# Reordering weight pieces, biases and operand copies around the middle of a two-layer fp32 kernel

## The chip, the cores and the metric

One core of a Trainium2 chip runs the whole program. The metric is the device time of one execution in microseconds (us), lower is better.

## The reference

```
x = x + ffn0(cond(x, c, W0c))      # cond: einsum('bct,bcd->bdt', x, W[c]), 64x64 matrices chosen by c
x = x + ffn1(cond(x, c, W1c))
ffn0(y) = y @ ternary(w) + b       # ternary(w) = where(|w| < 0.05, 0, sign(w)) * mean|w| of the column
ffn1(y) = y @ Wq.T + bias + 4 * (y @ A.T) @ B.T
Wq = NF4_LEVELS[q_weight] * q_scale          # one scale for 64 neighbours, 1024 x 1024
```

x is 32 x 64 x 1024 in fp32, `c` has 32 indices below 16, both weight matrices are 1024 x 1024, and A has 8 rows. Both layers run over the whole of x.

## The kernel before, in words

The 2048 rows of x are cut into NT = 16 tiles of 128 rows. Layer 0 handles tiles g = 0 to 15 and layer 1 handles the same tiles as g = 16 to 31. A tile passes through these steps:

- `mixed(g)`, 8 matmuls of 128 x 128 on TensorE that the trace shows as 16, multiplies the tile by its conditioning matrices and turns it, in two halves, into the PSUM tensor `xT`. There is one `xT` for almost all tiles, so `mixed(g+1)` waits until both halves of tile g have been read out of it.
- `high_x(g, h)` on ScalarE copies half h of it to SBUF in the reduced precision fp32r (`hh`), and `low_x(g, h)` on VectorE stores what that copy leaves over (`hl`, from PSUM minus `hh`). The two together are the left operand of the matmuls.
- `main(g, n)` on TensorE multiplies the operand by column half n of the weights (16 matmuls of 128 x 512 in layer 0, 24 in layer 1) into one of four PSUM banks, `bank_of(q)` with q = 2g + n.
- `leave_y(q)` on VectorE scales a finished bank into `ys` (layer 0) or adds it to x (layer 1). On GpSimd `add_bias(g)` adds the bias to the whole tile x, 128 x 1024, and `result(g)`, or `result_half(q)` for the first four tiles, adds `ys`.

Tiles 0 to 3 (F = 4) have an order written out by hand, since the ternary weights are being made meanwhile. From g = 4 on, TensorE repeats: `mixed(g+1)`, `main(g,0)`, `main(g,1)`. The text calls each `main(g,n)` a half slot m = 2g + n; ScalarE and VectorE are programmed by the same half slots.

Beside layer 0 the weights of layer 1 are made in 16 pieces d, each 128 x 512. A piece needs 9 ScalarE steps (`lines`: one integer conversion and 8 straight lines, six of them into the two buffers of `spare`), 6 VectorE steps (`maxima`, each reading a line), and on GpSimd `weight(d)`: a subtraction (line 584 of the trace) and a multiplication by the scales (line 589). Then TensorE turns the piece, `turn_w(d)`, with four transposes and one LoRA matmul (lines 1204 and 1206), into PSUM bank 3; ScalarE copies it (`high_w`) and VectorE stores the remainder (`low_w`). `turn_w(d)` waits for `weight(d)` and for `low_w(d-1)`. A planner spreads lines and maxima over half slots by `share`; `ready_in(d)` is the half slot in which the maxima of d end and `turned_in(d)` the one behind whose `main` TensorE turns it. In the kernel before these are

```
d          0  1  2  3  4  5  6  7  8  9 10 11 12 13 14 15
ready_in   4  8  9 11 12 14 15 17 18 20 21 23 24 26 27 28
turned_in  8  9 10 12 13 15 16 18 19 21 22 24 25 27 28 29
```

`weights_of(m)` on GpSimd runs `weight(d)` for the pieces with `ready_in(d) == m`, between the biases and results. The shares of the two engines are rounded apart: the last maximum that VectorE has in half slots 11 (a maximum of piece 4), 13 (piece 5) and 19 (piece 9) reads a line that ScalarE makes as the first of half slots 12, 14 and 20.

In half slots 32 to 39 (tiles 16 to 19) VectorE also makes sums of weight blocks (`sums_of_blocks`) for the last 12 tiles, which are multiplied in pairs with 7 instead of 8 block products (`PRODUCTS`, each with its bank). SyncE issues the loads and stores in one fixed order; `load_x(g+3)` stands behind loads of the quantized weights and behind the store of an earlier tile.

Of the kernel before, what the change touches and what calls it, by code (L numbers as in the profile page):

```python
# [26 lines left out]
F32 = mybir.dt.float32  # L27
# [3 lines left out]
ALU = mybir.AluOpType  # L31
ACT = mybir.ActivationFunctionType

P = 128
# [50 lines left out]
def build(nc, x, itok, mix0, w0, b0, mix1, q_weight, q_scale, b1, lora_a, lora_b, out):  # L85
# [18 lines left out]
    NT = B * C // P  # L104
# [37 lines left out]
    BLOCK = (B11, B12, B22, B21)  # L142

    A12, A11, S1, S2, S3, S4, A22 = range(7)
    PRODUCTS = ((A12, B21, 3), (A11, B11, 0), (S1, T1, 1), (S2, T2, 2), (S3, T3, 3), (S4, B22, 0),
                (A22, T4, 1))
    NPR = len(PRODUCTS)


# [20 lines left out]
    def sums_by(m):  # L170

        return NTS * HB * (m - NH * NT) // (NH * (SB - NT))

    def ready_in(d):

        return next(m for m in range(NH * NT) if share(2 * NC * ND, m + 1) >= 2 * NC * (d + 1))

    def turned_in(d):

        return max(NH * F, ready_in(d) + 1)  # L180

    def bank_of(q):
        if q >= NH * NT:
            return (q + 3) % F
        return q % F if q < 2 * F else (q - 2 * F) % 3

    def had_bank(q):
# [3 lines left out]
    with ExitStack() as ctx:  # L191
        def sb(name, shape, dt, until=ctx):
            return until.enter_context(nc.sbuf_tensor(name, shape, dt))
# [13 lines left out]
        ys = sb("ys", [P, F, BANK], F32)  # L207
        col_scale = sb("col_scale", [P, T], F32)
        bias = sb("bias", [P, T], F32)
        mix = sb("mix", [P, NM, P], F32)  # L210
        loraA = sb("loraA", [P, T], F32R)
        loraB = sb("loraB", [P, T], F32R)
# [49 lines left out]
        def x_of(g):  # L262

            if g < F:
                return x_first[:, g, :]
            return X[:, g % XS, :]
# [159 lines left out]
        def _(sp):  # L426
# [19 lines left out]
            def spill(t):  # L446

                tile_done(sp, t)
                sp.dma_start(out_v[t], x_of(t)).then_inc(s_spill[t] if t < F else s_left[t % XS], 16)
# [51 lines left out]
            for g in range(F, NT):  # L501
                load_mix(g + 3)
                for d in range(3, ND):
                    if d > 3 and ready_in(d - 3) // NH == g or d == 3 and g == F:
                        load_q(d)
                if g == F:
                    for t in range(F):
                        spill(t)
                else:
                    spill(g - 1)  # L510
                    load_x(g + 3)
            sp.wait_ge(s_xb, NT)
            sp.dma_start(bias[:, :], b1.rearrange("(a f) -> a f", a=1).to_broadcast([P, T])
                         ).then_inc(s_b1, 16)
            for g in range(NT, SB):
                load_mix(g + 3)
                if g == NT:
# [28 lines left out]
        def _(pool):  # L546
            def add_bias(g):
                arrived(pool, g)
                pool.wait_ge(s_b1 if g >= NT else s_b0, 16)
                pool.wait_ge(s_xT, NH * (g + 1))  # L550
                pool.tensor_tensor(x_of(g), x_of(g), bias[:, :], ALU.add).then_inc(s_xb, 1)  # L551

            def result_half(q):
                t, n = q % F, q // F
# [36 lines left out]
            def weights_of(m):  # L591
                for d in range(ND):
                    if ready_in(d) == m:
                        weight(d)
# [9 lines left out]
            def add_sum(p, i):  # L604
# [14 lines left out]
            add_bias(1)  # L619
            result_half(1)  # L620
            pool.wait_ge(s_scales, 16)
            pool.wait_ge(s_ah, 1)
            pool.wait_ge(s_res0, 2)
            pool.tensor_tensor(loraA[64:P, :], a_raw[64:P, :], loraA[64:P, :].bitcast(F32),
                               ALU.subtract).then_inc(s_al, 1)
            pool.wait_ge(s_al, 1)
            weights_of(0)
            add_bias(2)
            weights_of(1)
            result_half(2)  # L630
            weights_of(2)
            add_bias(3)
            weights_of(3)
            result_half(3)
            result_half(F)
            weights_of(4)
            result_half(F + 1)
            weights_of(5)
            add_bias(F)
            weights_of(6)  # L640
            result_half(F + 2)
            weights_of(7)
            for g in range(F, SB):
                if g == F:
                    result_half(F + 3)
                elif g <= NT:
                    result(g - 1)
                weights_of(NH * g)
                add_bias(g + 1)
                weights_of(NH * g + 1)  # L650
            low_side(0, 1)
# [16 lines left out]
        def _(act):  # L668
            def high_x(g, h):
                act.wait_ge(s_xT, NH * g + h + 1)  # L670
                if g >= F and h == 0:
                    act.wait_ge(s_acc, F + g - 3 if g < F + 2 else NH * (g - 1))
                act.activation(high(g)[:, h * HB:(h + 1) * HB, :], turned(g, h), ACT.Copy  # L673
                               ).then_inc(s_hh, 1)
# [55 lines left out]
            def high_sums(start, stop):  # L730

                for u in range(start, stop):
                    j, step = divmod(u, NTS)
                    for c, at in COMPLETE:
                        if step + 1 == at:
                            act.wait_ge(s_T, u + 1)
                            if u + 1 == COMPLETE[0][1]:
                                for t in range(F):
                                    act.wait_ge(s_spill[t], 16)
                            act.activation(w1(0, c, j), t_plain(c), ACT.Copy).then_inc(s_Th, 1)  # L740
# [41 lines left out]
            def left_S(p):  # L782
                copy_A21(p)
                for i in range(1, 5):
                    high_S(p, i)
                high_A(p, A22, 1)
# [46 lines left out]
            for g in range(SB):  # L833
                if g == 1:
                    colscale(1)
                if g == 2:
                    for h in range(NH):
                        act.wait_ge(s_bT, h + 1)
                        act.activation(loraB[:, h * BANK:(h + 1) * BANK], flat(h), ACT.Copy
                                       ).then_inc(s_loraB, 1)  # L840
                for m in (NH * g, NH * g + 1):
                    for d in range(ND):
                        if turned_in(d) == m - 1:
                            high_w(d)
                    if F - 1 <= g < SB - 1:
                        high_x(g + 1, m % NH)
                    elif m == NH * SB - 2:
                        left_A(0)
                    if g < NT:
                        lines(share(per, m), share(per, m + 1))  # L850
                    else:
                        high_sums(sums_by(m), sums_by(m + 1))
            left_S(0)
            for p in range(NP):
                copy_product(p)
# [5 lines left out]
        def _(dve):  # L861
# [7 lines left out]
            def ternary(n, k):  # L869
                i = n * KB + k  # L870
                if k in SIGNED:
                    dve.wait_ge(s_abs, n * KB + ABS.index(k) + 1)
                else:
                    dve.wait_ge(s_win[i], 16)
                    need(dve, s_T0, i - 1)
                    dve.tensor_scalar(spare[:, i % 2, :], w_raw(k, n), -THRESHOLD, None, ALU.is_le
                                      ).then_inc(s_neg, 1)
                    dve.wait_ge(s_neg, n * len(BOTH) + BOTH.index(k) + 1)
                dve.scalar_tensor_tensor(T0[:, n, k, :], w_raw(k, n), THRESHOLD, spare[:, i % 2, :],
                                         ALU.is_ge, ALU.mult if k in SIGNED else ALU.subtract  # L880
                                         ).then_inc(s_T0, 1)
# [163 lines left out]
            leave_y(1)  # L1045
            for k in range(4, KB):
                ternary(1, k)
            leave_y(2)
            per = 2 * NC * ND
            for g in range(SB):  # L1050
                for m in (NH * g, NH * g + 1):
                    if g >= F:
                        leave_y(m - 1)
                    for d in range(ND):
                        if turned_in(d) == m - 1:
                            low_w(d)
                    if F - 1 <= g < SB - 1:
                        low_x(g + 1, m % NH)
                    elif m == NH * SB - 2:
                        low_A(0, A12, 1)  # L1060
                        low_A(0, A11, 0)
                    if g < NT:
                        maxima(share(per, m), share(per, m + 1))
                    else:
                        sums_of_blocks(sums_by(m), sums_by(m + 1))
                    if m == NH * SB - 1:
                        for i in range(1, 5):
                            sum_S(0, i)
                    if g < F and m % NH == 0:
                        leave_y(F - 1 + g)  # L1070
            leave_y(NH * SB - 1)
# [200 lines left out]
```

## Time and profile before

| | |
|---|---|
| median of 3 runs | 372.36 us (371.15 to 373.5) |
| the profiled execution | 371.03 us, of which the span of the trace is 369.2 us |
| mean granted TensorE clock | 0.994 of full speed |
| busy | PE 96%, VectorE (DVE) 66%, GpSimd (POOL) 62%, ScalarE (ACT) 46% |
| chain that ended last | PE 73%, DVE 10%, ACT 6%, issue 4%, POOL 4% |

Busy shares are means over stages of very different load. A start time in the trace is counted from the first instruction. In rows of the trace the number before `<-` in square brackets is idle time ahead of the instruction, with what released it.

### The profile page before, as it was taken

The page shows a single profiled execution, that of the slowest core. Times are in us where ns is not written, and L with a number is a line of the kernel's source. Part 1 is how long each engine was busy: PE and PEld are TensorE (multiplying, and loading weights), DVE is VectorE, ACT ScalarE, POOL GpSimd, SP SyncE. Part 2 cuts the span into 40 slices and gives each one's busy share as a digit, 9 for nine tenths or more (in the row PEclk, how much of TensorE's full clock was granted, in tenths as well). Part 3 has the DMA queues.
Part 4 walks back from the last instruction along what each step waited for, and adds up shares of the span by engine and source line. Part 5 has one row for each costly group of instructions (what it writes and reads, how often), then busy time and mean ns, then how long its engine had stood idle before and what let it go on. Part 6 is the DMA issues. An engine that isn't in the chain of part 4 may idle for free.

```text
span 369.2 us, 5527 instructions
## 1 busy us (share of the span) xinstructions
PE 354.6 (96%) x1832; PEld 299.9 (81%) x1832; DVE 243.3 (66%) x361; ACT 169.6 (46%) x302; POOL 228.3 (62%) x147
## 2 busy tenths in 40 slices
PE   7999987999999999998989999999999999999996
PEld 6788875878888888887868888888888888888885
DVE  4996457587997887974699999846155362544522
ACT  4775647678888778882021323504013040231300
POOL 0769999956886878667443302386468464685642
PEclk9999999899999999999999999999999999999999
DMA  7994400554246146333331133021405014150202
GB/s 212 309 306 142 148 22 29 193 211 146 96 167 199 45 156 216 117 114 114 127 119 57 61 120 114 18 101 62 174 36 180 22 70 166 57 175 4 114 30 85
DMA packets 27838, 44.63 MB, mean 121 GB/s; under 512 B 8834, under 2 KB 17026, under 8 KB 27810
## 3 DMA queue, kind: packets, MB, share of 16 engines
q1 hardware_dynamic: 26466, 43.95, 34.9%
q10 hardware_dynamic: 1344, 0.33, 0.4%
q8 instruction: 15, 0.25, 0.3%
q14 instruction: 13, 0.11, 0.1%
HBM read 27.49 MB, written 16.78 MB: 120 GB/s over the span
## 4 chain that ended last, share of the span: by engine, by line
PE 73%; DVE 10%; ACT 6%; issue 4%; POOL 4%; DMA 1%; SPq 1%; DVEq 0%; POOLq 0%; ACTq 0%
PE acc L1177 31%; PE acc L1139 20%; PE xT L1103 9%; PE acc L1119 7%; PE spare L1103 3%; DVE plain_sums L927 3%; ACT spare L721 2%; POOL x_first L557 2%; DVE side_p L908 2%; DVE hl L865 2%; ACT hh L673 1%; PE acc L1204 1%; DMA mix<-in_L_cond_weights 1%; PE acc L1103 1%; POOL side_p L584 1%
## 5 line engine op out<-in xcount | busy, mean ns | idle before, releaser
L551 POOL TENSOR_TENSOR X<-X,bias 128x1024 f32<-128x1024 f32 x28 | 69.1, 2468 | 34.1 <-PE xT L1103 26.6
L1139 PE MATMUL acc<-T,hh 128*128 128x512 f32 x192 | 75.9, 396 | 0.0
L1139 PE MATMUL acc<-T,hl 128*128 128x512 f32 x192 | 75.0, 391 | 0.0
L721 ACT ACTIVATE spare<-q_mid 128x512 f32<-128x512 int8 x96 | 55.5, 596 | 13.6 <-DVE side_p L908 6.6
L1177 PE MATMUL acc<-W,hh 128*128 128x512 f32 x192 | 61.1, 389 | 0.0
L1103 PEld LDWEIGHTS xT<-mix,X 128*128 128x128 f32 x352 | 43.7, 197 | 7.4 <-issue 6.4
L1103 PE MATMUL xT<-mix,X 128*128 128x128 f32 x352 | 44.6, 282 | 4.2 <-DVE hl L865 4.1
L1010 DVE TENSOR_TENSOR X<-X,acc 128x512 f32<-128x512 f32 x36 | 24.7, 687 | 32.9 <-PE acc L1177 18.6
L1177 PEld LDWEIGHTS acc<-W,hh 128*128 128x128 f32 x192 | 36.0, 188 | 7.5
L1139 PEld LDWEIGHTS acc<-T,hl 128*128 128x128 f32 x192 | 36.1, 188 | 7.4
L1139 PEld LDWEIGHTS acc<-T,hh 128*128 128x128 f32 x192 | 36.1, 188 | 7.0
L1139 PE MATMUL acc<-W,hh 128*128 128x512 f32 x128 | 40.8, 393 | 0.0
L609 POOL TENSOR_TENSOR X<-X,ys 128x512 f32<-128x512 f32 x18 | 22.6, 1287 | 28.6 <-DVE ys L999 28.6
L1177 PE MATMUL acc<-W,hl 128*128 128x512 f32 x96 | 37.3, 389 | 0.0
L563 POOL TENSOR_TENSOR X<-X,ys 128x1024 f32<-128x1024 f32 x12 | 29.3, 2443 | 10.5 <-DVE ys L894 10.4
L584 POOL TENSOR_TENSOR side_p<-side_p,side_n 128x512 f32<-128x512 f32 x16 | 20.6, 1288 | 13.2 <-DVE side_n L908 13.1
L1139 PEld LDWEIGHTS acc<-W,hh 128*128 128x128 f32 x128 | 24.1, 188 | 4.9
L750 ACT ACTIVATE hh<-xT 128x512 fp32r<-128x512 f32 x12 | 6.5, 594 | 46.7 <-PE xT L1103 46.7
L673 ACT ACTIVATE hh<-xT 128x512 fp32r<-128x512 f32 x34 | 20.1, 590 | 14.9 <-PE xT L1103 14.7
L600 POOL TENSOR_TENSOR side_S<-plain_sums,side_S 128x512 fp32r<-128x512 f32 x6 | 7.8, 1301 | 30.4 <-ACT side_S L767 30.4
L894 DVE TENSOR_TENSOR ys<-acc,col_scale 128x512 f32<-128x512 f32 x32 | 21.8, 684 | 6.3 <-PE acc L1139 5.6
L908 DVE TENSOR_TENSOR side_p<-side_p,spare 128x512 f32<-128x512 f32 x32 | 21.9, 684 | 6.1 <-ACT spare L721 4.1
(97 smaller groups left out, 662.5 us busy)
## 6 DMA issues: line engine op xcount, KB each, us to landing
out<-X SPq DMA_DIRECT2D x26, 512.0 KB, 3.1
X<-out SPq DMA_DIRECT2D x16, 512.0 KB, 3.4
X<-in_x SPq DMA_DIRECT2D x12, 512.0 KB, 3.4
q_raw<-in_L_ffn_q_weight SPq DMA_DIRECT2D x16, 256.0 KB, 2.9
w_in<-in_L_ffn_w SPq DMA_DIRECT2D x15, 256.0 KB, 5.2
x_first<-in_x SPq DMA_DIRECT2D x4, 512.0 KB, 5.2
out<-x_first SPq DMA_DIRECT2D x4, 512.0 KB, 5.8
out<-X SPq DMA_DIRECT2D x4, 256.0 KB, 2.0
```

The costliest lines, as they stand in the source:

```text
L551: pool.tensor_tensor(x_of(g), x_of(g), bias[:, :], ALU.add).then_inc(s_xb, 1)
L563: pool.tensor_tensor(x_of(g), x_of(g), ys[:, at:at + NH, :].rearrange("p a f -> p (a f)"), ALU.add).then_inc(s_res0, NH)
L584: pool.tensor_tensor(lev, lev, side_n[:, :], ALU.subtract).then_inc(s_lev, 1)
L609: pool.tensor_tensor(t, t, sum_of(which), ALU.add).then_inc(s_sum2, 1)
L673: act.activation(high(g)[:, h * HB:(h + 1) * HB, :], turned(g, h), ACT.Copy).then_inc(s_hh, 1)
L721: act.activation(dst, q_mid[:, parity, :], ACT.Copy, scale=slope, bias=offset).then_inc(s_line, 1)
L908: ins = dve.tensor_tensor(dst, dst, spare[:, c % LR, :], ALU.max)
L1010: dve.tensor_tensor(t, t, bank, ALU.add).then_inc(s_take, 1)
L1103: mm = pe.matmul(turned(g, k // HB)[:, k % HB, :], x_of(g)[:, k * P:(k + 1) * P], mix[:, g % NM, :], start=True, stop=True)
L1119: mm = pe.matmul(acc[:, bank_of(q), :], a[:, k, :], T0[:, n, k, :], start=(k == 0 and j == 0), stop=(k == KB - 1 and j == 1))
L1139: mm = pe.matmul(acc[:, bank_of(q), :], a[:, k, :], b, start=(k == 0 and j == 0), stop=(k == KB - 1 and j == len(terms) - 1))
L1177: mm = pe.matmul(acc[:, bank, :], a[:, k, :], w1(part, c, k), start=(k == 0 and j == 0), stop=(k == HB - 1 and j == len(terms) - 1))
```

## The change

Piece 0 of the weights and piece 1 move up in GpSimd's order, ahead of biases and results of tiles 3, 4 and 5. The subtraction that makes the low part of `loraA` moves from GpSimd to VectorE. Both operand halves of a tile are made at the start of the even half slot (for tile 4, at the end of half slot 6). The second bias gets its own buffer, `bias1`, and is loaded in the iteration of tile 4 instead of after the last layer-0 bias. Piece 15 is turned behind half slot 30 instead of 29, and the bank order of layer 1 is turned by one so that bank 3 is not written by `main` until q = 35 (it was q = 32).

```
 PRODUCTS = banks (3, 0, 1, 2, 3, 0, 1)  ->  (0, 1, 2, 3, 0, 1, 2)

 def turned_in(d):
-    return max(NH * F, ready_in(d) + 1)
+    return max(NH * F, ready_in(d) + (2 if d == ND - 1 else 1))
 def bank_of(q):
     if q >= NH * NT:
-        return (q + 3) % F
+        return q % F

 # SyncE, iteration g == F, behind the four spills
+    sp.dma_start(bias1[:, :], b1 ...).then_inc(s_b1, 16)
 # SyncE, behind the loop over layer 0
-    sp.wait_ge(s_xb, NT)
-    sp.dma_start(bias[:, :], b1 ...).then_inc(s_b1, 16)

 # GpSimd
     add_bias(1)
     result_half(1)
     pool.wait_ge(s_scales, 16)
-    pool.wait_ge(s_ah, 1)
-    pool.wait_ge(s_res0, 2)
-    pool.tensor_tensor(loraA[64:P, :], a_raw[64:P, :], loraA[64:P, :] ..., ALU.subtract)
-    pool.wait_ge(s_al, 1)
-    weights_of(0)
     add_bias(2)
-    weights_of(1)
     result_half(2)
-    weights_of(2)
+    for m in range(NH * F - 3):          # piece 0
+        weights_of(m)
     add_bias(3)
-    weights_of(3)
     result_half(3)
     result_half(F)
-    weights_of(4)                        # piece 0
+    add_bias(F)
     result_half(F + 1)
-    weights_of(5)
-    add_bias(F)
-    weights_of(6)
+    for m in range(NH * F - 3, NH * F + 1):   # piece 1
+        weights_of(m)
     result_half(F + 2)
-    weights_of(7)
     for g in range(F, SB):
         if g == F:
             result_half(F + 3)
         elif g <= NT:
             result(g - 1)
-        weights_of(NH * g)
+        if g > F:
+            weights_of(NH * g)
         add_bias(g + 1)
         weights_of(NH * g + 1)

 # ScalarE (high_x) and, with the same lines, VectorE (low_x), in half slot m of tile g
-    if F - 1 <= g < SB - 1:
-        high_x(g + 1, m % NH)
+    if F <= g < SB - 1 and m % NH == 0:
+        high_x(g + 1, 0)
+        high_x(g + 1, 1)
     ... lines or maxima of the half slot ...
+    if m == NH * F - 2:
+        high_x(F, 0)
+        high_x(F, 1)

 # VectorE, ahead of leave_y(2)
+    dve.wait_ge(s_ah, 1)
+    dve.tensor_tensor(loraA[64:P, :], a_raw[64:P, :], loraA[64:P, :] ..., ALU.subtract)
```

## Rows read from the trace of the kernel before

**Rows 1.** TensorE's waits: us in total, times, the longest.
```profile
PE xT L1103 <- DVE hl L865: 4.1, 3, 1.8
PE acc L1204 <- POOL side_p L589: 3.9, 2, 2.6
```

**Rows 2.** Timeline of TensorE: start us, duration us, instruction.
```profile
51.30 2.02 PE L1103 MATMUL xT<-mix,X 128*128 128x128 f32 x16 [1.66 <-DVE hl L865]
...
63.94 0.74 PE L1204 MATMUL acc<-ident,side_p 128*128 128x128 f32 x4 [2.62 <-POOL side_p L589]
...
76.81 2.02 PE L1103 MATMUL xT<-mix,X 128*128 128x128 f32 x16 [0.60 <-DVE hl L865]
...
86.66 0.60 PE L1204 MATMUL acc<-ident,side_p 128*128 128x128 f32 x4
...
96.41 0.60 PE L1204 MATMUL acc<-ident,side_p 128*128 128x128 f32 x4
...
106.86 1.95 PE L1103 MATMUL xT<-mix,X 128*128 128x128 f32 x16
...
168.87 0.66 PE L1204 MATMUL acc<-ident,side_p 128*128 128x128 f32 x4 [1.29 <-POOL side_p L589]
...
193.30 2.02 PE L1103 MATMUL xT<-mix,X 128*128 128x128 f32 x16 [1.78 <-DVE hl L865]
```

**Rows 3.** The chain of waits: start us, us on the chain, what.
```profile
65.11 3.12 PE xT L1103 x16
...
86.82 0.44 PE acc L1204 x4
...
87.49 1.78 PE xT L1103 x16
```

**Rows 4.** Windows: the last three are granted TensorE clock, DMA share, GB/s.
```profile
64.00:66.00 2.00, 2.00 (x11) 1.91 (x12) 1.79 (x3) 1.54 (x3) 2.00 (x1) 0.59 0.00 0
```

**Rows 5.** Timeline of GpSimd, 40 to 64 us and the wait at 180.
```profile
41.92 2.39 POOL L624 TENSOR_TENSOR loraA<-a_in,loraA 64x1024 fp32r<-64x1024 f32 x1 [0.17 <-POOL x_first L557]
...
59.00 2.54 POOL L557 TENSOR_TENSOR x_first<-x_first,ys 128x512 f32<-128x512 f32 x2
...
62.84 1.05 POOL L589 TENSOR_TENSOR side_p<-side_p,scales 128x512 f32<-128x512 f32 x1
...
180.80 2.40 POOL L551 TENSOR_TENSOR X<-X,bias 128x1024 f32<-128x1024 f32 x1 [7.31 <-DMA bias<-in_L_ffn_bias]
```

**Rows 6.** Timeline of VectorE around tile 4 and 5.
```profile
38.99 1.48 DVE L908 TENSOR_TENSOR side_p<-side_p,spare 128x512 f32<-128x512 f32 x2 [3.08 <-ACT spare L721]
...
43.59 1.48 DVE L908 TENSOR_TENSOR side_n<-side_n,spare 128x512 f32<-128x512 f32 x2 [1.93 <-ACT spare L721]
...
56.28 1.48 DVE L908 TENSOR_TENSOR side_n<-side_n,spare 128x512 f32<-128x512 f32 x2
```

**Rows 7.** Timeline of ScalarE: both halves of tile 16.
```profile
170.68 0.60 ACT L673 ACTIVATE hh<-xT 128x512 fp32r<-128x512 f32 x1 [0.29 <-PE xT L1103]
171.58 0.60 ACT L673 ACTIVATE hh<-xT 128x512 fp32r<-128x512 f32 x1 [0.29 <-PE xT L1103]
```

**Rows 8.** Timeline of VectorE in half slot 12, ending with `low_x`.
```profile
79.10 0.69 DVE L908 TENSOR_TENSOR side_p<-side_p,spare 128x512 f32<-128x512 f32 x1 [0.45 <-ACT spare L721]
...
80.31 0.68 DVE L865 TENSOR_TENSOR hl<-xT,hh 128x512 fp32r<-128x512 f32 x1
```

**Rows 9.** Timeline of GpSimd: the last steps of pieces 4 and 5.
```profile
85.22 1.05 POOL L589 TENSOR_TENSOR side_p<-side_p,scales 128x512 f32<-128x512 f32 x1
...
94.86 1.05 POOL L589 TENSOR_TENSOR side_p<-side_p,scales 128x512 f32<-128x512 f32 x1
```

**Rows 10.** One VectorE line: count, min/median/max ns, first and last start.
```profile
L927 DVE TENSOR_TENSOR plain_sums<-plain_sums,W x12: 681/692/2773, 183.8 to 232.8; 128x512 f32<-128x512 f32 x12
```

**Rows 11.** Timeline of SyncE's queue: the load of tile 10.
```profile
102.70 0.34 SPq L434 DMA_DIRECT2D X<-in_x  x1
```

**Rows 12.** The page's DMA issues: KB each, median us to landing.
```profile
X<-in_x SPq DMA_DIRECT2D x12, 512.0 KB, 3.4
```

More of the change, by code:

```diff
@@ L144, in build @@
     A12, A11, S1, S2, S3, S4, A22 = range(7)
-    PRODUCTS = ((A12, B21, 3), (A11, B11, 0), (S1, T1, 1), (S2, T2, 2), (S3, T3, 3), (S4, B22, 0),
-                (A22, T4, 1))
+    PRODUCTS = ((A12, B21, 0), (A11, B11, 1), (S1, T1, 2), (S2, T2, 3), (S3, T3, 0), (S4, B22, 1),
+                (A22, T4, 2))
     NPR = len(PRODUCTS)
@@ L209, in build @@
         bias = sb("bias", [P, T], F32)
+        bias1 = sb("bias1", [P, T], F32)
         mix = sb("mix", [P, NM, P], F32)
@@ L508, in _ @@
                         spill(t)
+                    sp.dma_start(bias1[:, :], b1.rearrange("(a f) -> a f", a=1).to_broadcast([P, T])
+                                 ).then_inc(s_b1, 16)
                 else:
@@ L511, in _ @@
                     load_x(g + 3)
-            sp.wait_ge(s_xb, NT)
-            sp.dma_start(bias[:, :], b1.rearrange("(a f) -> a f", a=1).to_broadcast([P, T])
-                         ).then_inc(s_b1, 16)
             for g in range(NT, SB):
@@ L550, in add_bias @@
                 pool.wait_ge(s_xT, NH * (g + 1))
-                pool.tensor_tensor(x_of(g), x_of(g), bias[:, :], ALU.add).then_inc(s_xb, 1)
+                pool.tensor_tensor(x_of(g), x_of(g), (bias1 if g >= NT else bias)[:, :], ALU.add
+                                   ).then_inc(s_xb, 1)
             def result_half(q):
@@ L621, in _ @@
             pool.wait_ge(s_scales, 16)
-            pool.wait_ge(s_ah, 1)
-            pool.wait_ge(s_res0, 2)
-            pool.tensor_tensor(loraA[64:P, :], a_raw[64:P, :], loraA[64:P, :].bitcast(F32),
-                               ALU.subtract).then_inc(s_al, 1)
-            pool.wait_ge(s_al, 1)
-            weights_of(0)
             add_bias(2)
-            weights_of(1)
             result_half(2)
-            weights_of(2)
+            for m in range(NH * F - 3):
+                weights_of(m)
             add_bias(3)
-            weights_of(3)
             result_half(3)
             result_half(F)
-            weights_of(4)
+            add_bias(F)
             result_half(F + 1)
-            weights_of(5)
-            add_bias(F)
-            weights_of(6)
+            for m in range(NH * F - 3, NH * F + 1):
+                weights_of(m)
             result_half(F + 2)
-            weights_of(7)
             for g in range(F, SB):
@@ L1047, in _ @@
                 ternary(1, k)
+            dve.wait_ge(s_ah, 1)
+            dve.tensor_tensor(loraA[64:P, :], a_raw[64:P, :], loraA[64:P, :].bitcast(F32),
+                              ALU.subtract).then_inc(s_al, 1)
             leave_y(2)
@@ L1056, in _ @@
                             low_w(d)
-                    if F - 1 <= g < SB - 1:
-                        low_x(g + 1, m % NH)
+                    if F <= g < SB - 1 and m % NH == 0:
+                        low_x(g + 1, 0)
+                        low_x(g + 1, 1)
                     elif m == NH * SB - 2:
@@ L1068, in _ @@
                             sum_S(0, i)
+                    if m == NH * F - 2:
+                        low_x(F, 0)
+                        low_x(F, 1)
                     if g < F and m % NH == 0:
```

## The prediction

> **What bounds the kernel now.** The table of the profile comes first: TensorE is busy 96% of the span, the next engine 66%, and 73% of the chain that ended last is TensorE's. So a gain can only come from TensorE's gaps, and a loss only from new ones. TensorE's waits name them [rows 1]: 4.1 us in three waits of `mixed` for `low_x`, which must empty `xT`, and 3.9 us in two waits of `turn_w` for `weight` on GpSimd. (Start-up waits, for the identity and the first DMAs, are untouched.) The timeline places them [rows 2]: tile 5's `mixed` at 51.30 (1.66 us), `turn_w(1)` at 63.94 (2.62), tile 7's `mixed` at 76.81 (0.60), `turn_w(15)` at 168.87 (1.29), tile 18's `mixed` at 193.30 (1.78). Then the chain, for what a gap costs behind itself: a `mixed` that nothing held up takes 1.78 us of it, the one behind the long wait 3.12 [rows 3], and the windows say why: the granted clock there is 0.59 [rows 4], so much of that stretch ran at 1.2 instead of 2.4 GHz after TensorE had stood still for 2.62 us. The other gaps, up to 1.78 us, are followed by a `mixed` of 2.02 us [rows 2], so by 0.24 us of restart and no such fall.
>
> **Pieces 0 and 1 first on GpSimd.** Today the order is: low part of `loraA` (2.39 us, at 41.92), bias, result half, bias, two result halves, piece 0, and so on until two result halves at 59.00 that end at 61.54, and only then piece 1, ready at 62.84 + 1.05 = 63.89 [rows 5]. TensorE takes it at 63.94. Piece 1's maxima ended at 56.28 + 1.48 = 57.76 [rows 6], so it is GpSimd's order that is late, by 3.7 us. New order: a bias is 2.40 us (the row at 180.80), a result half 2.54 / 2 = 1.27, a piece 63.89 - 61.54 = 2.35 [rows 5]. From 41.92: bias 2, half, 45.6; piece 0, whose maxima end at 43.59 + 1.48 = 45.07 [rows 6], until 48.0; bias, three halves' worth and bias (2 x 2.40 + 3 x 1.27), 56.6; piece 1 must wait for its maxima at 57.76 and is ready at 60.1. TensorE wants it at 63.94 - 2.62 = 61.3, or 61.0 with what tile 5 gains. The margin is about 1 us and the wait goes. Its worth: 2.62, plus 3.12 - 1.78 = 1.34 on `mixed`, plus the turn itself, which took 65.11 - 63.94 = 1.17 to `mixed` and takes 87.49 - 86.82 = 0.67 at full clock [rows 2, 3], 0.50: **4.46 us**. What is queued behind piece 0: biases and results of tiles 3 to 5. Result half 3, which `leave_y(7)` needs, comes at 48.0 + 2.40 + 1.27 = 51.7, no later than now since the 2.39 us of `loraA` left the same queue.
>
> **`loraA` on VectorE.** A 128 x 512 step costs 0.69 there (row at 79.10 [rows 8]); twice the columns, at most 1.4 us, at about 33 us. Behind it are `leave_y(2)` and the first maximum; VectorE then sits idle for 3.08 us before 38.99 [rows 6], which covers it. Cost 0; with a wait for GpSimd ahead of it, between 0 and 0.5. The trace shows such waits: a step with both inputs in SBUF takes 0.69 at the median and up to 2.77 [rows 10], and the first long ones start while GpSimd runs its op at 180.80 [rows 5]. The Trainium skill (SBUF — State Buffer, "Who interferes with whom") has a rule that speaks against this move: a VectorE op with two SBUF inputs and a GpSimd op that reads SBUF lock each other out for a whole instruction. GpSimd adds column sums just then, so by the rule the step is held up; the idle time hides that too.
>
> **Tile 4 and 5.** `low_x(4,1)` no longer sits in half slot 7, but both copies still follow `mixed(4)` and one maximum. TensorE still waits; I take 0.3 us of the 1.66 as gained, between 0 and 0.6 (one VectorE step less ahead of it).
>
> **Both halves in the even half slot.** `low_x(g+1,1)` now runs a half slot of about 5 us before TensorE needs `xT` again. So tile 7's wait (0.60 + 0.24 = **0.84**) and tile 18's (1.78 + 0.24 = **2.02**) go [rows 2]. Tile 18's came from six sums that VectorE ran ahead of `low_x(17,1)`. Nothing is late next there: the sums feed products some 40 us on.
>
> **Piece 15 a half slot later.** `turn_w(15)` moves behind the next `main`, 16 matmuls or about 3.7 us later, more than the 1.29 it waited: **1.4 us** with part of a restart (1.29 to 1.53). Its `low_w` is needed only by the last weight block of `main(16,0)`, a whole `main(15,1)` and a `mixed` on, over 5 us.
>
> **Bank order, `bias1`, its early load.** The rotation alone changes no distance between uses of a bank except q = 33 to 35, whose former owners left two slots ago: 0. The early load removes GpSimd's 7.31 us wait [rows 5], which stood beside TensorE's work: 0. It puts one issue and 512 KB into SyncE's queue at tile 4. The nearest margin is tile 10's load: issued at 102.70, 3.4 us to landing, 106.1, and `mixed(10)` starts at 106.86 [rows 2, 11, 12], 0.76 us. That load stands behind a load of quantized weights that waits for ScalarE, so it moves with ScalarE. I take 0, with up to 1.5 us as a loss.
>
> Gains: 4.46 + 0.84 + 2.02 + 1.4 + 0.3 = **9.0 us**.
>
> **What it costs.** ScalarE now starts the lines of an even half slot only behind the second half of `mixed`. With ScalarE in step with TensorE that half comes 171.58 - 170.68 = 0.90 us behind the first [rows 7]. And VectorE has one more `low_x` (0.68, or 0.6 from start to start) ahead of the maxima [rows 8]. Pieces whose maxima end in an even half slot and that are turned one slot on are then 1.5 us later relative to TensorE, if VectorE's last maximum of the slot before hangs on ScalarE's first line of this one. By the shares those are pieces 4, 5 and 9. Piece 4 was ready at 85.22 + 1.05 = 86.27 and wanted at 86.66: 0.39 us to spare; piece 5 at 95.91 and 96.41: 0.50 [rows 2, 9]. In piece 4 the blocked maximum starts at 79.10, 2.29 us behind `mixed(7)`; it would start at about 0.90 later, less a little slack, then `low_x` twice: 1.4 later, 1.0 us late. Piece 5: 1.5 - 0.50 = 1.0. Piece 9 and the others (8, 12, 13) have more room or no blocked maximum: 0.3 in all. New waits: 1.0 + 1.0 + 0.3 = **2.3 us**. They are shorter than the 1.29 that brought no fall of the clock. In odd half slots VectorE and ScalarE each have one step less, so the lag doesn't pile up. Bounds: 0 (the slack of both engines takes it) to 6 x 1.5 = 9 us (each of pieces 4, 5, 8, 9, 12, 13 waits the full 1.5).
>
> **Sum.** 9.0 - 2.3 = 6.7 us. The profiled execution is 371.03 us, which would become 364.3; the median of the three runs is 1.33 us above it, and against that 372.36 - 6.7 = **365.7 us**, 1.8% less.
>
> **Rivals.**
> First, the helpers absorb the later start: VectorE is idle a third of the span, and pieces 4 and 5 may be pulled by gaps I don't see. Then 372.36 - 9.0 = 363.4. For it: no wait in the slots between 77 and 168 shows today. Against it: the two margins of 0.39 and 0.50 are smaller than the 1.5 added.
> Second, the later lines hit more pieces, and tile 10's load: 2.3 grows to about 5.5, giving 372.36 - 9.0 + 5.5 = 368.9. For it: `turn_w(15)` waits today [rows 2] though TensorE hadn't stopped since 77 us, so the helpers have little reserve by the end of layer 0.
> Third, slower: the serial path of every even half slot (`mixed`, both copies on ScalarE, line, maximum, two `low_x`, maxima, `weight`) outgrows TensorE's 86.66 - 76.81 = 9.85 us for a `mixed`, two `main` and a turn [rows 2]. If all six pieces wait 1.5 us and one of the waits gets as long as the 2.62 us one, with its 1.84 us at half clock, the cost is 9.0 + 1.1 + 1.84 = 11.9, and the time 372.36 - 9.0 + 11.9 = 375.3. It decides once the average new wait passes 9.0 / 6 = 1.5 us.
> Fourth, the change doesn't do what it says: piece 1's maxima come later than today, since both copies of tile 5 now precede its last lines; then 1 to 2 us of the 2.62 stay and with them perhaps the slow clock, giving 368 to 370.
>
> **Chances.** Forecast 0.5; first rival 0.22; second 0.15; third 0.05; fourth 0.08. The range runs from 361.8 (the first rival with the spread of 1.2 us that the three runs show below their median, and somewhat more) to 369.3 (the second). About 1% is what a measurement of this kernel can tell from no change; that is below 368.6 for faster. The forecast and the first rival lie there with nearly all they have, the second and fourth in part: 0.80 faster, 0.15 same, 0.05 slower.
>
> **What would show it.** In the trace after: no wait of `turn_w(1)`, and granted clock 1.00 in the window that read 0.59; `weight(1)` ended by 60.5; a shorter wait of tile 5's `mixed`; no waits of `mixed` for `low_x` at tile 7 and 18; `turn_w(15)` without one. New: `turn_w` for pieces 4 and 5 with about 1 us each, released by `weight`. The prediction is wrong upward if such waits come at more than three pieces or a `mixed` waits for its tile's DMA, and downward if TensorE runs from tile 5 to the end without a gap.

## The result, and the profile after

| | before | after |
|---|---|---|
| median of the runs | 372.12 us (371.08 to 373.5, 6 runs) | 366.05 us (365.56 to 366.9, 6 runs) |
| profiled execution | 371.03 us | 365.65 us |
| span of its trace | 369.2 us | 363.9 us |
| mean granted clock | 0.994 | 1.0 |

The ratio is 0.984, with a 95% interval of 0.981 to 0.986: 1.6% faster, 6.1 us between the medians. The forecast was 365.7.

Lines have shifted: 1108 is `mixed` (1103 before), 1209 `turn_w` (1204), 586 and 591 the subtraction and the multiplication of `weight`, 863 `low_x`, 912 `low_w`. Against [rows 1], the waits of `mixed` for `low_x` fell from 4.1 us in three to 1.4 in one. The waits of `turn_w` for `weight` fell from 3.9 us in two to 2.0 in three, and one of 1.1 us for `low_w` is new. The timeline of TensorE after, with every wait of this kind behind 45 us:

```profile
51.30 2.02 PE L1108 MATMUL xT<-mix,X 128*128 128x128 f32 x16 [1.37 <-DVE hl L863]
...
82.66 0.66 PE L1209 MATMUL acc<-ident,side_p 128*128 128x128 f32 x4 [0.99 <-POOL side_p L591]
...
93.52 0.66 PE L1209 MATMUL acc<-ident,side_p 128*128 128x128 f32 x4 [0.89 <-POOL side_p L591]
...
123.87 0.65 PE L1209 MATMUL acc<-ident,side_p 128*128 128x128 f32 x4 [0.16 <-POOL side_p L591]
...
145.72 0.63 PE L1209 MATMUL acc<-ident,side_p 128*128 128x128 f32 x4 [1.11 <-DVE W L912]
```

Against [rows 2]: tile 5's `mixed` waits 1.37 instead of 1.66 us; the waits of `turn_w(1)`, tile 7, `turn_w(15)` and tile 18 are gone. The new ones belong to pieces 4, 5, 9 and 12. The chain of waits after shows `turn_w(1)` passed without a stop and tile 6's `mixed` at full speed (1.78 us, where [rows 3] had 3.12), and then how piece 4 is made:

```profile
61.35 0.44 PE acc L1209 x4
...
62.02 1.78 PE xT L1108 x16
...
71.89 1.80 PE xT L1108 x16
73.71 0.60 ACT hh L667
74.31 0.50 ACT spare L715
74.90 0.54 issue
75.58 0.46 issue
76.04 1.28 DVE hl L863 x2
...
79.41 0.70 DVE side_n L906
80.17 1.30 POOL side_p L586
81.56 1.05 POOL side_p L591
82.66 0.66 PE acc L1209 x4
```

It is a serial path through four engines: tile 7's `mixed`, the second copy on ScalarE, one line, VectorE's maximum and `leave_y` behind that line (mostly inside the two "issue" pieces), both `low_x`, four maxima (the last of them shown), the two steps of `weight`, and the turn. The pace on it from `mixed(7)` to the turn is 82.66 - 71.89 = 10.8 us, where TensorE's own work in between takes 86.66 - 76.81 = 9.85 [rows 2].

The window that had a granted clock of 0.59 [rows 4] is now at full clock, 2.4 GHz:

```profile
64.00:66.00 2.00, 2.00 (x11) 1.62 (x10) 2.00 (x5) 1.97 (x5) 2.00 (x2) 1.00 0.00 0
```

On GpSimd piece 1 ended at 59.02 + 1.05 = 60.07 instead of 63.89 us [rows 5], TensorE wanting it at 61.35; the LoRA step moved to VectorE took 1.23 us:

```profile
59.02 1.05 POOL L591 TENSOR_TENSOR side_p<-side_p,scales 128x512 f32<-128x512 f32 x1
```

```profile
33.24 1.23 DVE L1047 TENSOR_TENSOR loraA<-a_in,loraA 64x1024 fp32r<-64x1024 f32 x1 [0.90 <-ACT loraA L825]
```

That step was not stretched, but what GpSimd did beside it was. The three column sums that GpSimd runs there took 4.18 us before and 5.21 after:

```profile
30.13 4.18 POOL L577 TENSOR_TENSOR col_scale<-col_scale,w_in 128x512 f32<-128x512 f32 x3 [0.32 <-ACT w_in L686]
```

```profile
30.41 5.21 POOL L579 TENSOR_TENSOR col_scale<-col_scale,w_in 128x512 f32<-128x512 f32 x3 [0.33 <-ACT w_in L680]
```

The same three take 4.18 us in all four profiles with the subtraction on GpSimd, and 5.20 or 5.21 in all nine with it on VectorE. So the stretch set GpSimd's queue back by 1.0 us.

### The profile page after: what moved, and what is told of

The parts are those of the page before. It is cut to its first block, busy times and chain, and to the rows that moved or that the text cites. A ratio compares the mean times of both kernels' runs of the same rounds, so it can differ in the third digit from the quotient of the medians.

```text
span 363.9 us, 5526 instructions
## 1 busy us (share of the span) xinstructions
PE 352.1 (97%) x1832; PEld 298.1 (82%) x1832; DVE 237.8 (65%) x362; ACT 170.8 (47%) x302; POOL 224.8 (62%) x146
## 4 chain that ended last, share of the span: by engine, by line
PE 86%; DVE 4%; POOL 3%; issue 2%; ACT 2%; DMA 1%; SPq 1%; POOLq 0%; DVEq 0%; ACTq 0%
PE acc L1182 31%; PE acc L1144 29%; PE xT L1108 11%; PE acc L1124 7%; PE spare L1108 3%; PE acc L1209 2%; DMA w_in<-in_L_ffn_w 1%; POOL side_p L586 1%; PE acc L1211 1%; DVE hl L863 1%; POOL side_p L591 1%; DVE side_n L906 1%; ACT spare L715 1%; POOL X L565 1%; PE acc L1108 1%
## 5 line engine op out<-in xcount | busy, mean ns | idle before, releaser
L552 POOL TENSOR_TENSOR X<-X,bias 128x1024 f32<-128x1024 f32 x28 | 67.5, 2412 | 29.3 <-PE xT L1108 29.1
L1108 PEld LDWEIGHTS xT<-mix,X 128*128 128x128 f32 x352 | 42.6, 192 | 3.1 <-issue 1.8
L1108 PE MATMUL xT<-mix,X 128*128 128x128 f32 x352 | 42.9, 275 | 1.4 <-DVE hl L863 1.4
L906 DVE TENSOR_TENSOR side_n<-side_n,spare 128x512 f32<-128x512 f32 x32 | 21.9, 686 | 6.9 <-ACT spare L715 4.4
```

The source lines that it names most:

```text
L552: pool.tensor_tensor(x_of(g), x_of(g), (bias1 if g >= NT else bias)[:, :], ALU.add).then_inc(s_xb, 1)
L906: ins = dve.tensor_tensor(dst, dst, spare[:, c % LR, :], ALU.max)
L1108: mm = pe.matmul(turned(g, k // HB)[:, k % HB, :], x_of(g)[:, k * P:(k + 1) * P], mix[:, g % NM, :], start=True, stop=True)
```

## The experiments

Times are medians; each group was run with the kernel before on the same chip (its medians were 371.56, 371.52 and 372.63 us in the three groups, and 372.12 beside the changed kernel). Where a run is compared with the changed kernel, the two come from different groups. So where such a difference carries the argument two are given: that of the medians, and that of what each gains on the kernel before in its own group.

### First group: one part alone, one part undone

**Pieces and `loraA` alone**: the kernel before with

```
 # GpSimd: the new order of pieces 0 and 1, without the LoRA subtraction
 # VectorE, ahead of leave_y(2)
+    dve.wait_ge(s_ah, 1)
+    dve.tensor_tensor(loraA[64:P, :], ..., ALU.subtract)
```

> The kernel before with GpSimd's new order and the LoRA subtraction on VectorE alone; copies, piece 15, bank order and second bias as before. My theory: turn_w(1) stops waiting and the slow clock behind it goes, 4.5 us. The waits of mixed for low_x at tiles 7 and 18 and the wait of turn_w(15) stay. 372.1 - 4.5 = 367.6 us. Rival: the helpers lose their reserve as TensorE comes earlier and hand most of it back in later waits: 370 or more, with new waits of turn_w between 77 and 168 us.

Measured: 367.57 us, ratio 0.989 (0.985 to 0.993), 4.0 us less than before. The waits of TensorE:

```profile
68.20 0.66 PE L1199 MATMUL acc<-ident,side_p 128*128 128x128 f32 x4 [0.28 <-POOL side_p L589]
...
165.48 0.66 PE L1199 MATMUL acc<-ident,side_p 128*128 128x128 f32 x4 [1.31 <-POOL side_p L589]
...
189.91 2.02 PE L1098 MATMUL xT<-mix,X 128*128 128x128 f32 x16 [1.78 <-DVE hl L857]
```

As my theory had it: `turn_w(1)` doesn't wait, and the three waits named (0.65 at tile 7, 1.31, 1.78 us) and tile 5's (1.67) stay to a few hundredths. New are 0.28 us at `turn_w(2)` and 0.18 at tile 13's `mixed`. Two thirds of the whole change's gain are in this one part.

**Both copies in the even half slot, alone**: the kernel before with

```
-    if F - 1 <= g < SB - 1:
-        high_x(g + 1, m % NH)              # and low_x on VectorE
+    if F <= g < SB - 1 and m % NH == 0:
+        high_x(g + 1, 0); high_x(g + 1, 1) # tile 4's at the end of half slot 6
```

> The kernel before with both operand halves in the even half slot alone. My theory: the waits for low_x at tiles 7 and 18 go (2.9 us), turn_w for pieces 4 and 5 wait about 1 us each, piece 15 (ready in an even slot, turned one later) waits 1 to 1.5 us more than its 1.29, and turn_w(1) still waits over 2 us: 372.1 plus or minus 1. Rival: the copies cost nothing and only empty xT earlier: 369.2, and no new wait of turn_w.

Measured: 374.0 us, ratio 1.006 (1.003 to 1.008): alone, this part makes the kernel slower. It was worse than I expected, 372.1 give or take 1. The profile has all the waits named and one of size that I hadn't: `turn_w(12)`, 1.06 us for `low_w`.

```profile
64.91 0.72 PE L1212 MATMUL acc<-ident,side_p 128*128 128x128 f32 x4 [2.95 <-POOL side_p L589]
...
87.96 0.66 PE L1212 MATMUL acc<-ident,side_p 128*128 128x128 f32 x4 [1.01 <-POOL side_p L589]
...
151.01 0.63 PE L1212 MATMUL acc<-ident,side_p 128*128 128x128 f32 x4 [1.06 <-DVE W L918]
...
173.75 0.66 PE L1212 MATMUL acc<-ident,side_p 128*128 128x128 f32 x4 [2.34 <-POOL side_p L589]
...
174.48 3.50 PE L1111 MATMUL xT<-mix,X 128*128 128x128 f32 x16
```

The rival (copies are free) is out: the same waits for pieces 4, 5 (0.89) and 12 stand here without GpSimd's new order. Piece 15's wait grew from 1.29 to 2.34 us, which is why this part needs the next. And that wait cost more than its length: behind it the granted clock fell a second time, and the next `mixed` took 3.50 us, where one that nothing held up takes 1.95 [rows 2].

```profile
176.00:178.00 2.00, 2.00 (x11) 2.00 (x10) 0.69 (x1) 0.60 (x1) 2.00 (x2) 0.50 0.00 0
```

My expectation had the wait and not this fall, which in this profile costs about 1.5 us.

**The copies put back**: the changed kernel with the lines just shown undone.

> The changed kernel with the copies put back, one half in each half slot. My theory: the new waits of turn_w for pieces 4, 5, 9 and 12 (3.15 us in the changed kernel's profile) go, and the waits for low_x at tiles 7, 13 and 18 return (about 3.2 us with their restarts): 366 plus or minus 0.7, the same time by other waits. Rival: the new waits come from GpSimd's order or from TensorE being early, not from the copies: they stay, and 369 us.

Measured: 364.55 us, ratio 0.981 (0.976 to 0.985), 7.0 us less than before where the change as a whole took 6.1. The new waits of pieces 4, 5, 9 and 12 went, as expected. But of those that should have come back one is missing:

```profile
73.50 2.02 PE L1100 MATMUL xT<-mix,X 128*128 128x128 f32 x16 [0.66 <-DVE hl L859]
...
164.97 2.02 PE L1100 MATMUL xT<-mix,X 128*128 128x128 f32 x16 [0.71 <-DVE hl L859]
```

Tile 5 (1.67) and tile 7 wait again as before; tile 13 (0.16) and tile 16 wait a little, which they did not do to speak of before; tile 18 doesn't wait at all. So something else in the change also cures tile 18's wait, and my expectation of 366 was 1.5 us too high for that. VectorE's timeline behind tile 17's `low_x` shows what:

```profile
177.19 1.67 DVE L921 TENSOR_TENSOR plain_sums<-W 128x512 f32<-128x512 f32 x1
178.89 3.49 DVE L921 TENSOR_TENSOR plain_sums<-plain_sums,W 128x512 f32<-128x512 f32 x2
182.30 0.69 DVE L921 TENSOR_TENSOR plain_sums<-W 128x512 f32<-128x512 f32 x1
183.02 1.29 DVE L921 TENSOR_TENSOR plain_sums<-plain_sums 128x512 f32<-128x512 f32 x2
```

The six block sums take 7.1 us. In the kernel before the first three alone took 8.4 (2.7 to 2.8 us each, against 0.69 [rows 10]):

```profile
181.00 2.73 DVE L927 TENSOR_TENSOR plain_sums<-W 128x512 f32<-128x512 f32 x1
183.78 5.58 DVE L927 TENSOR_TENSOR plain_sums<-plain_sums,W 128x512 f32<-128x512 f32 x2
```

Before, GpSimd ran three 128 x 1024 adds back to back beside them, from 180.80 to 188.81 us: tile 16's bias, which had waited for its DMA [rows 5], tile 15's result and tile 17's bias. Here tile 16's bias ran at 170.18 us, and only the other two are left beside the sums, until 181.10.

**Piece 15 behind half slot 29 again**: in the changed kernel

```
-    return max(NH * F, ready_in(d) + (2 if d == ND - 1 else 1))
+    return max(NH * F, ready_in(d) + 1)
```

> The changed kernel with piece 15 turned behind half slot 29 again. My theory: weight(15) ends at 168.4 us in the changed kernel and TensorE would want it at 165.9, so a wait of 2.5 us, more than the 1.29 of before since the piece's half slot is even and its maxima now follow both copies. 368.6 us if the clock holds, up to 370.4 if it falls to 1.2 GHz as behind the 2.62 us wait. Rival: the wait is that of before, 1.3 us: 367.4.

Measured: 368.32 us, ratio 0.993 (0.990 to 0.995).

```profile
169.56 0.66 PE L1209 MATMUL acc<-ident,side_p 128*128 128x128 f32 x4 [2.32 <-POOL side_p L591]
```

A wait of 2.32 us, and 2.3 us more than the changed kernel between the medians (2.8 if each is set against its own kernel before): my theory. In the profiled execution the clock held (the windows from 168 to 174 us all have 1.00), but not in all. Three of the nine executions have a mean granted clock of 0.994 to 0.995, as the kernel before has with its one fall, and took 369.25 to 370.33 us, within my bound for a fall; five took 367.99 to 368.32. The ninth, the profiled one, took 369.30 with the clock at 1.0; it has two start-up waits of 1.4 us for a DMA.

### Second group: the second bias, and another place for the second copy

**One bias buffer**: the changed kernel with `bias1` gone and the load behind `sp.wait_ge(s_xb, NT)`, as before.

> The changed kernel with the second bias loaded late into the first one's buffer, as before. My theory since the split-halves run: tile 18's wait for low_x has two independent cures, the copies in the even half slot and the early bias (which takes a 128 x 1024 GpSimd add away from VectorE's block sums). With the copies still in the even slot the late bias costs nothing: 366.05 plus or minus 0.5, no wait of mixed at tile 18, though the block sums are slow again (2.7 us instead of 0.7 for three of them). Rival: the sums reach TensorE by another way, and it is 367.5 or more.

Measured: 366.54 us, ratio 0.986 (0.984 to 0.989); no wait at tile 18. VectorE's sums in the same place:

```profile
181.05 2.89 DVE L925 TENSOR_TENSOR plain_sums<-W 128x512 f32<-128x512 f32 x1
183.97 5.57 DVE L925 TENSOR_TENSOR plain_sums<-plain_sums 128x512 f32<-128x512 f32 x2
```

Three of them are long again, and no `mixed` waits, as both `low_x` are already done. The profile has one idle stretch of TensorE that the changed kernel lacks, 0.72 us at 234.6 us with no releaser shown; whether the late bias causes it isn't known.

**Early second bias alone**: the kernel before with

```
+    # SyncE, iteration g == F, behind the spills
+    sp.dma_start(bias1[:, :], b1 ...).then_inc(s_b1, 16)
-    sp.wait_ge(s_xb, NT)
-    sp.dma_start(bias[:, :], b1 ...).then_inc(s_b1, 16)
```

> The kernel before with the second bias in its own buffer and loaded at tile 4, nothing else. My theory: tile 18's wait of 1.78 us goes with its restart and the small ones of tiles 19 and 20, 2.0 to 2.5 us, all else stays: 372.0 - 2.2 = 369.8. Rival, my prediction's own costing (the early load is worth 0, since GpSimd's 7.31 us wait lay beside TensorE's work): 372.0, with the 1.78 us wait still there.

Measured: 368.77 us, ratio 0.991 (0.989 to 0.994), 2.75 us less than before. The timeline of TensorE keeps the waits at tile 5 (1.67), `turn_w(1)` (2.67), tile 7 (0.62) and `turn_w(15)` (1.32); there is none behind it. VectorE's block sums take the same 7.1 us as in the run with the copies put back. The prediction's own costing of this edit, 0, is wrong by more than 2 us, and its reason for it too: GpSimd's 7.31 us wait cost nothing by itself, but it moved a GpSimd add on top of VectorE's sums. Tile 18's wait had two independent cures in this change, and either is enough.

**Second copy last**: the changed kernel, but in layer 0

```
     if F <= g < SB - 1 and m % NH == 0:
         high_x(g + 1, 0)                    # and low_x on VectorE
-        high_x(g + 1, 1)
+        if g >= NT - 1:
+            high_x(g + 1, 1)
     ... lines or maxima of the half slot ...
+    if F <= g < NT - 1 and m % NH == 0:
+        high_x(g + 1, 1)
```

> The changed kernel, but in layer 0 (from tile 5 on) the second half's copies stand at the end of the even half slot, behind its lines and maxima, instead of ahead of them; from tile 16 on as in the changed kernel. My theory: the lines no longer wait for the whole mixed and the maxima not for a second low_x, so the new waits of pieces 4, 5, 9 and 12 go (3.15 us and restarts), and xT is still emptied half a slot or more before TensorE needs it, so tile 7's wait doesn't return: 366.05 - 3.3 = 362.7. Rival: VectorE reaches the second low_x no sooner than with the halves split over two slots, and the waits of mixed at tiles 7, 13 and 16 (0.66, 0.16 and 0.71 us there) return: 364.5.

Measured: 362.96 us, ratio 0.977 (0.975 to 0.979). Two waits are left behind 45 us, tile 5's (1.36) and this:

```profile
142.62 0.63 PE L1215 MATMUL acc<-ident,side_p 128*128 128x128 f32 x4 [0.96 <-DVE W L915]
```

Pieces 4, 5 and 9 don't wait, and no `mixed` from tile 6 on does. Piece 12's wait for `low_w(11)` stays, against my expectation. VectorE's timelines say where it comes from. By the shares, the last maximum of half slot 24 (the first of piece 13) reads the first line of half slot 25, which ScalarE makes behind `high_w(11)`; `low_w(11)` stands behind that maximum. In the changed kernel, in the one with the copies put back, and in this one:

```profile
143.68 0.69 DVE L902 SCALAR_TENSOR_TENSOR side_p<-side_p,spare 128x512 f32<-128x512 f32 x1 [1.27 <-ACT spare L715]
...
144.89 0.68 DVE L912 TENSOR_TENSOR W<-acc,W 128x512 fp32r<-128x512 f32 x1
```

```profile
141.84 0.69 DVE L898 SCALAR_TENSOR_TENSOR side_p<-side_p,spare 128x512 f32<-128x512 f32 x1 [1.84 <-ACT spare L715]
...
143.04 0.68 DVE L908 TENSOR_TENSOR W<-acc,W 128x512 fp32r<-128x512 f32 x1
```

```profile
139.98 0.69 DVE L905 SCALAR_TENSOR_TENSOR side_p<-side_p,spare 128x512 f32<-128x512 f32 x1 [1.76 <-ACT spare L715]
140.59 0.68 DVE L866 TENSOR_TENSOR hl<-xT,hh 128x512 fp32r<-128x512 f32 x1
```

Counted from the start of `turn_w(11)` (140.13, 139.35 and 137.15 us), the maximum starts 3.55, 2.49 and 2.83 us on, and `low_w(11)` 4.76, 3.69 and 4.64 us on. So in the changed kernel the maximum itself is 1.06 us late. In this one it is 0.34 us late, and the second `low_x`, now between it and `low_w(11)`, adds 0.60. The two sums fit the waits of 1.11 and 0.96 us.

**Tile 4's copies first**: the same, with `low_x(4, 0)` and `low_x(4, 1)` ahead of VectorE's maximum of half slot 6.

> The kernel of the run before, with VectorE's two copies of tile 4 ahead of its one maximum of half slot 6 instead of behind it. That maximum reads a line which ScalarE makes only behind both of its copies. My theory: tile 5's mixed then doesn't wait 1.37 us but 0.3 or less, 1.2 us with part of the restart: 361.4. Rival: the maximum that comes later delays piece 1, turn_w(1) waits instead, and nothing is gained: 362.7.

Measured: 363.16 us, ratio 0.977 (0.975 to 0.980): no gain over the run before it. Tile 5's wait is gone, `turn_w(2)` waits 0.23 us, and `turn_w(1)` waits 1.11 us for `low_w(0)`:

```profile
61.67 0.63 PE L1215 MATMUL acc<-ident,side_p 128*128 128x128 f32 x4 [1.11 <-DVE W L915]
```

It came by another way than the rival had it. VectorE, now at `leave_y(7)` a step and more earlier, stood still there for result half 3, which comes from GpSimd's queue no sooner than before:

```profile
53.81 0.69 DVE L895 TENSOR_TENSOR ys<-acc,col_scale 128x512 f32<-128x512 f32 x1 [1.74 <-POOL x_first L559]
```

### Third group: sizes

**`loraA` back on GpSimd**, in the changed kernel, ahead of tile 2's bias:

> The changed kernel with the subtraction for the low part of loraA back on GpSimd, ahead of tile 2's bias. My theory: its 2.4 us push the whole queue behind it. Result half 3, for which leave_y(7) already waits 0.62 us, and piece 1 come 2.4 us later; piece 1 was ready at 60.07 and TensorE wants it at 61.35, so turn_w(1) waits at least 1.1 us, and up to 3 as leave_y(7) holds VectorE: 367.2 to 370.5, 368.5 the likeliest. Rival, if moving it was beside the point: piece 1 had 1.3 us to spare and the queue has gaps: 366.05.

Measured: 367.47 us, ratio 0.986 (0.982 to 0.990). That is 1.4 us more than the changed kernel between the medians, 0.9 if each is set against its own kernel before, and less than the 368.5 that I took as likeliest. GpSimd's queue gets 2.4 us of work and has back the 1.0 us by which its column sums are shorter here. `turn_w(1)` waits, not for piece 1 but for `low_w(0)`, since `leave_y(7)` holds VectorE for 2.27 us, where it was 0.62. The two waits that the changed kernel lacks sum to 1.3 us:

```profile
62.48 0.63 PE L1211 MATMUL acc<-ident,side_p 128*128 128x128 f32 x4 [0.65 <-DVE W L917]
69.47 0.66 PE L1211 MATMUL acc<-ident,side_p 128*128 128x128 f32 x4 [0.68 <-POOL side_p L591]
```

**Piece 0 behind result half 3**, in the kernel with tile 4's copies first:

```
-    for m in range(NH * F - 3):
-        weights_of(m)
     add_bias(3)
     result_half(3)
+    for m in range(NH * F - 3):
+        weights_of(m)
```

> The kernel with tile 4's copies first, and piece 0 on GpSimd behind result half 3 instead of ahead of tile 3's bias. There leave_y(7) waited 1.74 us for result half 3, low_w(0) came late and turn_w(1) waited 1.11 us. My theory: result half 3 comes 2.4 us earlier, leave_y(7) doesn't wait, turn_w(1) neither, and piece 0, ready near 53.7, is still ahead of the turn at 56.1: 363.16 - 1.3 = 361.9. Rival: the line that needs piece 0's subtraction is late now, piece 1's maxima with it, and turn_w(1) waits as long for piece 1: 363.2.

Measured: 362.69 us, ratio 0.973 (0.969 to 0.977). `leave_y(7)` no longer waits, and neither does `turn_w(1)` for `low_w(0)`, but it came out 0.8 us above the expected 361.9: `turn_w(1)` waits 0.47 us for piece 1, and `turn_w(2)` 0.88. The wait has been pushed from `mixed(5)` to the next thing in GpSimd's queue twice; that queue is full from 47 to 72 us in this run, so its sum of work, and no longer its order, seems to bound the stretch; no run tested that. This kernel and the two it builds on (362.96 and 363.16 us) are the fastest of the study, and their intervals overlap.

**Only VectorE's second copy last**, ScalarE's both first, in the changed kernel:

> The changed kernel with VectorE's second copy of a tile at the end of the even half slot (layer 0 from tile 5 on), while ScalarE still makes both of its copies first. My prediction split the delay of an even-slot piece into 0.90 us (ScalarE waiting for the second half of mixed) and 0.6 us (VectorE's second step). By that the waits of turn_w for pieces 4 and 5 fall from 0.99 and 0.89 to about 0.4 and 0.3, and the time is 366.05 - 1.3 = 364.7. Rival A, VectorE's step is all of it: no waits, as with both copies moved, 363.0. Rival B, ScalarE's wait is all of it: 366.05.

Measured: 365.08 us, ratio 0.979 (0.975 to 0.983), 1.0 us less than the changed kernel between the medians (1.5 by the groups).

```profile
83.63 0.66 PE L1212 MATMUL acc<-ident,side_p 128*128 128x128 f32 x4 [0.62 <-POOL side_p L591]
...
93.90 0.66 PE L1212 MATMUL acc<-ident,side_p 128*128 128x128 f32 x4 [0.29 <-POOL side_p L591]
```

Piece 4's wait fell by 0.37 and piece 5's by 0.60 us when VectorE's step was out of the way, and to nothing when ScalarE's copy was too; both rivals are out. VectorE's 0.6 us holds for piece 5, roughly for piece 4. Of ScalarE's 0.9 the runs show only that it is at least the 0.62 and 0.29 us that were left, since a wait can't fall below nothing. Piece 12's wait fell too, from 1.11 to 0.83.

## Why the prediction was right, point by point

The forecast of 365.7 us stands against 366.05, and a gain of 6.7 against 6.1. The large waits went and came back where the prediction said. But some of its steps were wrong in cause or size, and the total came so close in part by luck: the two errors that matter most, `bias1` and the cause of tile 18's wait, cancel in it.

- **Pieces first, 4.46 us**: right. From the same 51.30 us start of tile 5's `mixed`, tile 6's ends at 62.02 + 1.78 = 63.80 after and at 65.11 + 3.12 = 68.23 before [rows 3], 4.43 us. Alone it gave 4.0. Piece 1 was ready at 60.07, predicted 60.1, but that match is luck. The prediction had GpSimd free at 56.6 and waiting for maxima until 57.76; in the trace the maxima end at 57.27 and GpSimd, later than reckoned, gets to the piece at 57.63.
- **`loraA` on VectorE, cost 0**: right for TensorE; it took 1.23 us (at most 1.4 predicted) and the first maximum it delays fits in the idle time. The step that failed is "no later than now" for result half 3, forecast at 51.7 us. GpSimd's column sums took 1.0 us longer beside the moved step, result half 3 ended at 52.8, and `leave_y(7)` waited 0.62 us for it instead of 0.21. The prediction had looked for a hold-up on VectorE only; it fell on GpSimd, and the margin of 1.3 us in front of `turn_w(1)` covered it. That the step had to leave GpSimd is shown by the run that puts it back, 0.9 to 1.4 us slower.
- **Tile 5, 0.3 us**: 1.66 to 1.37, right; 1.36 or 1.37 stands in every run that has the copies moved with the maximum ahead of them, 1.66 or 1.67 in every one that has not.
- **Tile 7, 0.84 us**: right; the wait is gone and comes back (0.66) with the copies split.
- **Tile 18, 2.02 us**: the time was right, the cause only half. I gave it to the even-slot copies; the early second bias does it as well, by itself.
- **`bias1`, 0**: wrong. As a part alone it is worth 2.75 us between the medians (2.3 to 4.3 by the interval of the ratio). In the sum this cancelled, because its effect and that of the copies overlap. The step that failed is "which stood beside TensorE's work: 0": I looked at the wait and not at what the instructions behind it would stand next to. The prediction had even named the long sums beside that GpSimd add. The rows it cites for them start at 183.8, behind the end of the add at 183.20; the sum that does stand beside it is the one at 181.00 above.
- **Piece 15, 1.4 us**: right, with the note that the reference point moves. With the copies in the even slot the unmoved turn would wait 2.32 us, so it is worth 2.3 in this company, and more in an execution in which the clock then falls.
- **New waits 2.3 us**: pieces 4 and 5, predicted 1.0 and 1.0, measured 0.99 and 0.89; piece 9 within the "0.3 in all", 0.16. Missing was piece 12's, 1.11 us for `low_w(11)`. I had checked the slack of `weight(12)` alone, and not the second thing that `turn_w` waits for, `low_w(11)` behind a maximum that hangs on ScalarE. Also missing was the restart. I charged 0.24 us of it to each `mixed` wait that went and none to a wait that came, while a held turn takes 0.66 us on the chain and one that nothing held 0.44 (at 61.35). That is some 0.2 us for each of the four, 0.8 in all.
- **Rivals**: the first (helpers absorb all) is refuted by the two waits of about 1 us. The second had new waits of 5.5 us; 3.15 were measured against the forecast's 2.3, and tile 10's load, its bound of 1.5 us, never made TensorE wait. The third (a net loss by the even-slot path) is true of that part alone, 0.6% slower, but not of the sum. The fourth is out: piece 1's maxima end at 57.27, no later than the 57.76 of before.
- **The sign for "wrong upward"**, such waits at more than three pieces, was all but met: `turn_w` waits for `weight` at three pieces (4, 5, 9), and at a fourth, piece 12, for `low_w`. The time came out above the forecast, by 0.35 us.

The profiled execution came out at 365.65 us, 1.3 above the 364.3 of the sum. The new waits, 3.15 us with 0.8 of restarts, are 1.6 to 1.7 more than the 2.3 of the sum. What is left, 0.3 the other way, can't be placed in one profile: the longest start-up wait for a DMA alone is between 1.26 and 2.00 us in the profiles of this study.

So the even-slot copies are the one part of the change that costs more than it gives: without them it runs in 364.55 us (1.5 less between the medians, 0.9 if each is set against its own kernel before), and with the second copy behind the lines instead of ahead in 362.96 (3.1 less, or 2.5).

## What to carry to other kernels

When an in-order engine gets its work ordered earlier, ask for each step that moves what now stands behind it, and check every semaphore of the consumer, not the one that came last in the trace before, and ask what the other engines do beside a step that changes its engine. Two edits that cure the same wait must not be added, and a kernel with one undone tells them apart. A helper's long idle time may cost nothing and yet decide what its next instructions collide with.

## What the runs showed of the hardware

A VectorE step with both inputs in SBUF and a GpSimd step beside it can hold each other up. A block sum takes 0.69 us alone and up to 2.89 (the one-bias run) beside GpSimd's 128 x 1024 adds; those in turn go from 2.40 to 2.84 us in the changed kernel. With the `loraA` step it was GpSimd that lost, 1.03 us over three column sums, and VectorE's step that kept its 1.23. That is the sort of hold-up that the Trainium skill (SBUF — State Buffer, "Who interferes with whom") describes for two SBUF inputs against a reading GpSimd op. The trace agrees, and with the block sums it cost TensorE about 2 us through VectorE's queue.

```profile
179.12 2.84 POOL L552 TENSOR_TENSOR X<-X,bias 128x1024 f32<-128x1024 f32 x1
```

The granted clock fell behind waits of 2.62 us (before), 2.67 and 2.95 (the early bias and the even-slot copies alone), and behind the 2.34 us wait of piece 15 in that last run, but not behind 2.32 us in the profile of the run that turns piece 15 early. Nor does one kernel always do the same: three executions of the early-bias kernel have a mean granted clock of 0.995, and the fourth, the fastest (367.54 us), 1.0. So the length of the wait alone doesn't say whether the clock falls. With the copies alone, the window from 66 us, behind the 2.95 us wait, is wholly at the lower level, 1.2 GHz:

```profile
66.00:68.00 2.00, 2.00 (x12) 2.00 (x11) 1.90 (x4) 0.95 (x3) 1.92 (x2) 0.50 0.00 0
```
